# A decoder layer for 16 sequences on one core: first sequence's self attention in half head groups, gelu run twice in place of a cast, maxima of two heads in one transposed tile, and new instruction orders

## Chip, cores and metric

The kernel runs on one core of one Trainium2 chip. The metric is the device time of one launch in microseconds (us), of which the median of several runs is compared. TensorE is PE in the profile's rows, VectorE is DVE, ScalarE is ACT, GpSimd is POOL, and SyncE (SP) issues the DMAs.

## The reference, cut to what matters

One pre-norm decoder layer in float32 for 16 sequences of 256 tokens and 256 features: self attention with 16 heads of 16, cross attention to 77 context rows, and a soft mixture of experts with 8 experts of 128 slots and a hidden size of 1024.

```python
x = x + attn(layernorm(x))                 # softmax(q k^T / 16) v, then Wo
x = x + xattn(layernorm(x), ctx, ctx)      # softmax(q k^T / 4) v, then Wo
xn, se = rms_norm(layernorm(x), gamma_x), rms_norm(slot_embeds, gamma_slot)
logits = einsum('bsd,etd->bset', xn, se)   # 256 tokens x 1024 slots
dispatch = softmax(logits, axis=1)         # over tokens
slots = einsum('bsd,bset->betd', xn, dispatch)
h = gelu(slots @ w1, approximate=False)    # 1024 x 1024
processed = h @ w2
combine = softmax(logits.reshape(b, s, e * t), axis=-1)
x = x + einsum('bnd,bsn->bsd', processed, combine)
```

## The kernel before

**Steps and batches.** A batch is one sequence. Its work is cut into steps with names such as `scores`, `mt`, `shifted`, `ex` and `hidden`, and each engine has its own list of steps. A step name carries a letter for the stage: `c` is self attention, `d` is cross attention and the logits, `m` is the mixture of one batch, `l` is the tail of the mixture. `START` lists the steps of the first pass (self attention of batches 0, 1 and 2, cross attention of 0 and 1, mixture of 0), `ORDER` is the loop body, run 13 times with `c` at batch b+2, `d` at b+1, `m` at b and `l` at b-1, and `FINISH` is the tail. The lists are written out and fix the order on every engine. The engines meet through semaphores that the steps count up and wait on, so a late step holds everything behind it on its engine.

**Matrix products.** The large products are made from three products each of float32 numbers split in two parts, `hi` and `lo`: hi x hi, lo x hi and hi x lo (L453 to L455, one instruction each). ScalarE writes the `hi` part out of PSUM and VectorE or GpSimd subtracts it to make `lo`.

**PSUM.** There are eight banks of 128 x 512. Bank 0 serves the small products of all stages one after another (transposes, `pv`, output projections, keys of the context). Banks 1 to 4 serve a group of four heads' scores and the logits; bank 5 slots, bank 6 and 5 hidden (`hidden_bank`), bank 7 the products `outer` and `combine`.

**Self attention.** A batch has four groups (`quads`, n = 0 to 3) of four heads, on four groups of 32 rows of the array. For each: `scores.n` fills banks 1 to 4; VectorE's `mx.n` takes the maximum of each row (L1122, 2048 elements a partition) and splits it in two; `mt.n` transposes these (L550); `sh.n` adds them to the queries' tile `qz` (L1133), so that `shifted.n` computes keys by queries less the maximum into the same banks (L561); `ex.n` takes the exponent of all four banks into `pt` (L879); `pv.n` multiplies with the values (L574). `scores.n+1` waits for `ex.n`. After `pv.3` come `ml.1`, the normalisation `nrm` (a sum, a reciprocal, two shuffles, two products) and `oproj` (L585). Cross attention does the same with groups of eight heads, `scores2` to `pv2`, in two rounds; there the maxima of even and odd heads lie in two tiles, so `mt2` is four transposes (L638).

**Mixture.** Per batch there are four chunks c of 256 slots. `dispatch.c`, `slots.c`, four steps `hidden.c.q` (12 products each), `outer.c.0` and `outer.c.1` (24 each), `combine.c`. Behind each `hidden.c.q` ScalarE's `ge` writes gelu to `h_f` (L959), VectorE's `hid` casts it to `h_hi` (L1332) and GpSimd's `hid` subtracts in place to `h_lo` (L1456), which `outer` waits for. `hidden.c.2` and `hidden.c.3` wait for the `ge` of two steps earlier, since there are two banks. ScalarE loads a table when it goes from an exponent to gelu or back (L959 and L929 ACT_TABLE_LOAD).

**Fillers.** `idle.n` issues n float32 products of the identity with itself into bank 7 (L811, two records each in the trace), where TensorE would wait otherwise; only in `START`.

## Time and profile before

| what | value |
|---|---|
| runs | 1713.97, 1714.13, 1718.77 us; median 1714.13 us |
| profiled execution, its own time | 1718.86 us |
| its span (first to last instruction) | 1717.1 us |
| mean granted TensorE clock | 0.989 |
| TensorE busy | 1633.2 us, 95% |
| VectorE busy | 1287.0 us, 75% |
| ScalarE busy | 979.1 us, 57% |
| GpSimd busy | 540.1 us, 31% |

The profiled execution took 4.7 us more than the median of the runs, 0.3%. Busy shares are means over the whole span. A matrix product's record is longer than the distance to the next one, since products overlap, so the distance between starts is what a step costs TensorE.

### The profile page before, as it was taken

What the parts mean: (1) busy time and instruction counts of PE and PEld (TensorE: products, weight loads), DVE (VectorE), ACT (ScalarE), POOL (GpSimd) and SP (SyncE); (2) the same over time, 40 slices, a digit from 0 to 9 for tenths busy, and PEclk for the clock granted to TensorE, in tenths of its full rate; (3) what the DMA queues carried; (4) which work ended last, traced back from release to release, by engine and by line L of the source; (5) the groups of instructions that cost most, each with busy time, mean ns of one, the idle gap of its engine ahead of it and who ended that gap; (6) DMA issues with size and microseconds to landing.
All of it is one profiled execution on the core that took longest, in us unless ns stands there. A gap on an engine that the chain in (4) does not pass through costs nothing.

```text
span 1717.1 us, 37771 instructions
## 1 busy us (share of the span) xinstructions
PE 1633.2 (95%) x15552; PEld 1475.2 (86%) x15552; DVE 1287.0 (75%) x2778; ACT 979.1 (57%) x1505; POOL 540.1 (31%) x450
## 2 busy tenths in 40 slices
...
DMA packets 20843, 19.48 MB, mean 11 GB/s; under 512 B 9920, under 2 KB 19776, under 8 KB 20288
## 3 DMA queue, kind: packets, MB, share of 16 engines
...
q14 instruction: 47, 0.39, 0.1%
...
## 4 chain that ended last, share of the span: by engine, by line
PE 79%; DVE 9%; ACT 8%; issue 3%; POOL 1%; DMA 0%; DVEq 0%; SPq 0%; ACTq 0%
PE ps L453 20%; PE ps L454 18%; PE ps L455 18%; PE ps L574 3%; DVE mx L1122 2%; PE ps L561 2%; ACT pt L879 2%; PE ps L541 2%; PE ps L731 2%; PE ps L650 2%; PE ps L585 2%; PE ps L662 2%; PE ps L495 1%; ACT L959 1%; ACT h_f L959 1%
## 5 line engine op out<-in xcount | busy, mean ns | idle before, releaser
L1456 POOL TENSOR_TENSOR h_lo<-h_f,h_hi 128x512 fp32r<-128x512 f32 x256 | 336.3, 1321 | 462.0 <-DVE h_hi L1332 462.0
L453 PE MATMUL ps<-sl_hi,w_hi 128*128 128x256 f32 x1024 | 302.5, 295 | 6.0 <-DVE sl_lo L1014 3.8
L453 PE MATMUL ps<-w_hi,h_hi 128*128 128x256 f32 x1024 | 299.5, 292 | 7.5 <-POOL h_lo L1456 7.5
L454 PE MATMUL ps<-sl_hi,w_lo 128*128 128x256 f32 x1024 | 289.9, 283 | 0.0
L455 PE MATMUL ps<-sl_lo,w_hi 128*128 128x256 f32 x1024 | 289.9, 283 | 0.0
L454 PE MATMUL ps<-w_hi,h_lo 128*128 128x256 f32 x1024 | 289.7, 283 | 0.0
L455 PE MATMUL ps<-w_lo,h_hi 128*128 128x256 f32 x1024 | 289.6, 283 | 0.0
L453 PEld LDWEIGHTS ps<-sl_hi,w_hi 128*128 128x128 f32 x1024 | 196.1, 192 | 32.5 <-issue 16.5
L453 PEld LDWEIGHTS ps<-w_hi,h_hi 128*128 128x128 f32 x1024 | 196.1, 191 | 19.9 <-POOL h_lo L1456 18.3
L959 ACT ACTIVATE h_f<-ps 128x512 f32<-128x512 f32 x256 | 150.6, 596 | 104.6 <-PE ps L455 103.9
L1462 POOL TENSOR_TENSOR cb_lo<-ecomb,cb_hi 128x512 fp32r<-128x512 f32 x60 | 82.0, 1367 | 381.9 <-ACT ecomb L974 381.9
L454 PEld LDWEIGHTS ps<-sl_hi,w_lo 128*128 128x128 f32 x1024 | 196.6, 192 | 0.0
L454 PEld LDWEIGHTS ps<-w_hi,h_lo 128*128 128x128 f32 x1024 | 196.4, 192 | 0.1
L455 PEld LDWEIGHTS ps<-sl_lo,w_hi 128*128 128x128 f32 x1024 | 196.2, 192 | 0.0
L455 PEld LDWEIGHTS ps<-w_lo,h_hi 128*128 128x128 f32 x1024 | 196.1, 191 | 0.0
L1332 DVE CAST h_hi<-h_f 128x512 fp32r<-128x512 f32 x256 | 142.0, 565 | 40.5 <-ACT h_f L959 40.4
L1122 DVE TENSOR_REDUCE mx<-ps 128x8 f32<-128x2048 f32 x64 | 146.2, 2285 | 18.3 <-PE ps L541 18.3
L879 ACT ACTIVATE pt<-ps 128x2048 f32<-128x2048 f32 x64 | 120.1, 1877 | 51.3 <-PE ps L561 51.3
L825 ACT ACTIVATE ds_hi<-ps 128x512 fp32r<-128x512 f32 x64 | 38.2, 598 | 127.7 <-PE ps L731 127.7
L1014 DVE TENSOR_TENSOR ds_lo<-ps,ds_hi 128x512 fp32r<-128x512 f32 x64 | 44.0, 687 | 73.0 <-ACT ds_hi L825 72.9
L959 ACT ACT_TABLE_LOAD x67 | 86.0, 1283 | 15.4 <-PE ps L455 14.3
L825 ACT ACTIVATE lg<-ps 128x512 f32<-128x512 f32 x64 | 38.1, 597 | 92.0 <-PE ps L455 92.0
...
## 6 DMA issues: line engine op xcount, KB each, us to landing
...
```

What stands on the lines that cost most here:

```text
L453: te.matmul(o, lhs[0], rhs[0], start=first, stop=False)
L454: te.matmul(o, lhs[1], rhs[0], start=False, stop=False)
L455: return te.matmul(o, lhs[0], rhs[1], start=False, stop=last)
L574: last = te.matmul(ps[32 * i:32 * i + 32, 0, 0:S], vz[:, j, 8 * c + 2 * i + e, :], pt[:, i, j, :], start=j == 0, stop=j == NT - 1)
L825: return nc.scalar.activation(o, i, ACT.Copy)
L879: nc.scalar.activation(pt[:, :, :, :].rearrange("p i j s -> p i (j s)"), ps[:, 1:1 + R, :], ACT.Exp)\
L959: nc.scalar.activation(h_f[:, 2 * q:2 * q + 2, :], halves(hidden_bank(b, q)), ACT.Gelu).then_inc(s["ge"], 1)
L1014: return V.tensor_tensor(o, a, hi.bitcast(f32), ALU.subtract)
L1122: V.tensor_reduce(mx[:, n, :, :], ps[:, 1:1 + R, :].rearrange("p i (t s) -> p i t s", t=NT), AX, ALU.max, negate=True).then_inc(s["mx"], 1)
L1332: V.tensor_copy(h_hi[:, 2 * q:2 * q + 2, :], h_f[:, 2 * q:2 * q + 2, :]).then_inc(s["h_hi"], 1)
L1456: Q_.tensor_tensor(h_lo[:, part, :], h_f[:, part, :], h_hi[:, part, :].bitcast(f32), ALU.subtract)\
L1462: Q_.tensor_tensor(low[:, :, :], ecomb[:, :, :], hi[:, :, :].bitcast(f32), ALU.subtract).then_inc(s["cb_lo"], 1)
```

## The change

What the core of the diff does, part by part:

1. **Batch 0's self attention** goes by half groups: two heads a step, on one of three pairs of banks (1-2, 3-4, 5-6). `scores`, `mx`, `mt`, `sh`, `shifted` and `ex` get a second number, the half h. A second maxima tile `md_b` and a second `pt_odd` keep neighbours apart. Semaphores whose names begin with `h_` count the first halves.
2. **Normalisation in two parts** (`first_nrm`, `first_nrm2`) for batch 0's self and cross attention: each two groups are normalised by themselves, the first two while the others run.
3. **Gelu twice**: ScalarE writes gelu to `h_hi` and again to `h_f`; VectorE's 256 casts go, and GpSimd waits for ScalarE.
4. **Maxima of cross attention** go into one tile: `mt2` has two transposes in place of four. The masked queries are now made by GpSimd ahead of it (`qm`, two instructions a batch), and `sh2` adds the transposed maxima.
5. **The copy `res` goes** (`keep`): the sum after cross attention lies in two alternating tiles, `x2_even` and `x2_odd`.
6. **The slot embeddings' scaling** (3.6 us on GpSimd, once) goes to ScalarE as eight instructions, `se_mul`.
7. **All four lists** of `START` and `ORDER`, and those of `FINISH`, are new. `START` has fillers in more places: 206 products in place of 152.

```diff
@@ -430,6 +436,19 @@
 
             return (5, 6, 7)[k] if second_batch(a) else 1 + k
 
+        def pt_of(a, n):
+
+            return pt_odd if a == 0 and n % 2 else pt
+
+        def half_banks(n, h):
+
+            at = 1 + 2 * ((2 * n + h) % 3)
+            return slice(at, at + 2)
+
+        def half_sem(name, h):
+
+            return s[name] if h else s["h_" + name]
+
         def hidden_bank(b, q):
 
             return 1 + q if last_batch(b) else 6 - q % 2
...
+                    pe.wait_ge(s["q_sb"], 1)
+                    pe.wait_ge(s["k_lo"], 1)
+                u = 2 * n + h - 3
+                if u >= 0:
+                    pe.wait_ge(half_sem("ex", u % 2), u // 2 + 1)
+                for t in range(NT):
+                    for queries, keys, first in ((qs, k_hi, True), (qz, k_lo, False)):
+                        for i in range(2):
+                            rows = slice(32 * (2 * h + i), 32 * (2 * h + i) + 32)
+                            last = te.matmul(ps[:, half_banks(n, h).start + i, t * S:(t + 1) * S],
+                                             queries[rows, n, t * P:(t + 1) * P], keys[rows, n, :], start=first, stop=not first)
+                last.then_inc(half_sem("s_ps", h), 1)
 
+            def half_mt(n, h):
+
+                misc_free(f"c.mt.{n}.{h}", 0)
+                pe.wait_ge(half_sem("md", h), n + 1)
...
@@ -871,8 +935,18 @@
                 nc.scalar.activation(k_d[:, :, :], k_d[:, :, :], ACT.Identity, scale=half[:, 0:1], bias=half[:, 3:4])\
                     .then_inc(s["k_m"], 1)
 
-            def ex(a, n):
+            def half_ex(n, h):
 
+                act.wait_ge(half_sem("st_ps", h), n + 1)
+                if n >= 2:
+                    act.wait_ge(s["pv"], n - 1)
+                nc.scalar.activation(pt_of(0, n)[:, 2 * h:2 * h + 2, :, :].rearrange("p i j s -> p i (j s)"),
+                                     ps[:, half_banks(n, h), :], ACT.Exp).then_inc(half_sem("ex", h), 1)
+
+            def ex(a, n, *h):
+
+                if h:
+                    return half_ex(n, *h)
                 act.wait_ge(s["st_ps"], nth("st_ps", a, n + 1))
                 if n:
                     act.wait_ge(s["pv"], nth("pv", a, n))
+                nc.scalar.activation(h_hi[:, 2 * q:2 * q + 2, :], halves(hidden_bank(b, q)), ACT.Gelu)
                 nc.scalar.activation(h_f[:, 2 * q:2 * q + 2, :], halves(hidden_bank(b, q)), ACT.Gelu).then_inc(s["ge"], 1)
 
             def pr(b, c):
...
@@ -1116,8 +1198,33 @@
                     last = V.tensor_tensor(vz[:, :, e::2, e * HD:(e + 1) * HD], new[:, :, e::2, :], b_v[:, :, e::2, :], ALU.add)
                 last.then_inc(s["v_sb"], 1)
 
-            def mx_step(a, n):
+            def half_mx(n, h):
+
+                dve.wait_ge(half_sem("s_ps", h), n + 1)
+                of = slice(2 * h, 2 * h + 2)
+                top_sem, hi_sem, top_n, hi_n = (s["mx"], s["md_hi"], n + 1, n + 1) if h else (
+                    s["h_mx"], s["h_mx"], 2 * n + 1, 2 * n + 2)
+                V.tensor_reduce(mx[:, n, of, :], ps[:, half_banks(n, h), :].rearrange("p i (t s) -> p i t s", t=NT), AX,
+                                ALU.max, negate=True).then_inc(top_sem, 1)
+                dve.wait_ge(top_sem, top_n)
+                if n:
+                    dve.wait_ge(half_sem("mt_ps", h), n)
+                top = mx[:, n, of, :].rearrange("p i t -> p t i")
+                V.tensor_copy(md_of[h][:, :, of, HD].bitcast(f32r), top).then_inc(hi_sem, 1)
+                dve.wait_ge(hi_sem, hi_n)
+                V.tensor_tensor(md_of[h][:, :, of, HD + 1], top, md_of[h][:, :, of, HD], ALU.subtract).then_inc(half_sem("md", h), 1)
+
...
@@ -1142,8 +1251,24 @@
                 V.scalar_tensor_tensor(xo[:, c, :], odd, half[:, 1:2], xo[:, c, :], ALU.mult, ALU.add)\
                     .then_inc(s["ml"], 1)
 
-            def nrm(a):
+            def first_nrm(a, c):
+
+                step = "rl" if c else "la"
+                dve.wait_ge(s["ml"], nth("ml", a, 2 * c + 1))
+                V.stream_shuffle(od[:, c, :], lsum[:, c, :], [8 * c + HD * (1 - r // HD) for r in range(2 * HD)])\
+                    .then_inc(s["ls"], 1)
+                dve.wait_ge(s["ls"], nth("ls", a, c + 1))
+                V.reciprocal(od[:, c, :], od[:, c, :]).then_inc(s[step], 1)
+                dve.wait_ge(s[step], nth(step, a, 1))
+                dve.wait_ge(s["ml"], nth("ml", a, 2 * c + 2))
+                last = V.tensor_tensor(od[:, c, :], xo[:, c, :], od[:, c, :], ALU.mult)
+                if c:
...
-                    last = V.tensor_reduce(md2[:, :, e, :, HD * (1 - e)].rearrange("p t i -> p i t"), every[:, :, :, e, :],
+                    last = V.tensor_reduce(md2[:, :, :, HD * (1 - e)].rearrange("p t i -> p i t"), every[:, :, :, e, :],
                                            AX, ALU.max, negate=True)
                 last.then_inc(s["md2"], 1)
 
             def sh2_step(a, c):
 
                 dve.wait_ge(s["mt2_ps"], nth("mt2_ps", a, c + 1))
+                dve.wait_ge(s["q2_m"], nth("q2_m", a, 1))
                 for e in range(2):
-                    last = V.scalar_tensor_tensor(sh2[:, e, :], q2[:, c, :], half[:, e:e + 1],
-                                                  ps[:, 0, e * S:(e + 1) * S], ALU.mult, ALU.add)
+                    last = V.scalar_tensor_tensor(sh2[:, c, e, :], ps[:, 0, 0:S], half[:, 1 - e:2 - e],
+                                                  sh2[:, c, e, :], ALU.mult, ALU.add)
                 last.then_inc(s["sh2"], 1)
 
             def ml2(a, c):
...
@@ -1450,8 +1580,16 @@
                     last = Q_.tensor_scalar(kms2[:, :, e, :], km2[:, :, e, :], half[:, 4 + e:5 + e], None, ALU.add)
                 last.then_inc(s["kms2"], 1)
 
+            def qm(a):
+                pool.wait_ge(s["q2_sb"], nth("q2_sb", a, 1))
+                if later(a):
+                    pool.wait_ge(s["st2_ps"], nth("st2_ps", a - 1, C))
+                for e in range(2):
+                    last = Q_.tensor_scalar(sh2[:, :, e, :], q2[:, :, :], half[:, e:e + 1], None, ALU.mult)
+                last.then_inc(s["q2_m"], 1)
...
-        m.slots.2 m.outer.1.1 c.mt.1 m.hidden.2.0 c.shifted.1 m.hidden.2.1 c.scores.2 c.pv.1 m.hidden.2.2 m.hidden.2.3
+        m.slots.2 m.outer.1.1 c.mt.1 c.shifted.1 m.hidden.2.0 m.hidden.2.1 c.scores.2 c.pv.1 m.hidden.2.2 m.hidden.2.3
```

**TensorE in the first pass**, behind the first scores of batch 0. `md` holds the maxima, `qs`/`k_hi` and `qz`/`k_lo` the two parts of queries and keys, `consts` by itself is a filler. Before:

```order
L541 MATMUL ps<-k_lo,qz 128x256 x4
L811 MATMUL ps<-consts 128x128 x11
L550 MATMUL ps<-consts,md 128x128 [waits s_md,s_xt1_lo]
L550 MATMUL ps<-consts,md 128x128
L811 MATMUL ps<-consts 128x128
L561 MATMUL ps<-qs,k_hi 128x256 [waits s_sh]
L561 MATMUL ps<-qs,k_hi 128x256 x3
L561 MATMUL ps<-qz,k_lo 128x256 x4
L561 MATMUL ps<-qs,k_hi 128x256 x4
L561 MATMUL ps<-qz,k_lo 128x256 x4
```

After, the first half group's transposes and shifted scores, then the second's transposes:

```order
L875 MATMUL ps<-consts 128x128 x4
L590 MATMUL ps<-consts,md 128x128 [waits s_h_md,s_xt1_lo]
L590 MATMUL ps<-consts,md 128x128
L875 MATMUL ps<-consts 128x128 x6
L601 MATMUL ps<-qs,k_hi 128x256 [waits s_h_sh]
L601 MATMUL ps<-qs,k_hi 128x256
L601 MATMUL ps<-qz,k_lo 128x256 x2
L601 MATMUL ps<-qs,k_hi 128x256 x2
L601 MATMUL ps<-qz,k_lo 128x256 x2
L590 MATMUL ps<-consts,md_b 128x128 [waits s_md,s_h_sh]
L590 MATMUL ps<-consts,md_b 128x128
L875 MATMUL ps<-consts 128x128 x3
```

A step has half as many products, other halves stand between, and the fillers are cut in smaller pieces.

**ScalarE in the loop**, first chunk of the mixture, from the second gelu step to the exponent of cross attention (`q` and `k_d` belong to other stages, `edt` is the exponent for `dispatch`). Before:

```order
L959 ACTIVATE h_f<-ps 128x512 [waits s_h_ps]
L895 ACTIVATE q_109<-ps,bcol 128x256 [waits s_od2,s_q2_ps]
L895 ACTIVATE q_109<-ps,bcol 128x256
L825 ACTIVATE k_hi<-k_d 128x1024 [waits s_k_d]
L871 ACTIVATE k_d<-k_d,half 128x1024 [waits s_k_h]
L959 ACTIVATE h_f<-ps 128x512 [waits s_h_ps] x2
L929 ACT_TABLE_LOAD
L929 ACTIVATE edt,csum<-lg,cm 128x256 [waits s_cm]
L929 ACTIVATE edt,csum<-lg,cm 128x256
L906 ACTIVATE pt_114<-ps,mkc 77x2048 [waits s_st2_ps]
```

After:

```order
L1033 ACTIVATE h_hi<-ps 128x512 [waits s_h_ps]
L1034 ACTIVATE h_f<-ps 128x512
L1033 ACTIVATE h_hi<-ps 128x512 [waits s_h_ps]
L1034 ACTIVATE h_f<-ps 128x512
L889 ACTIVATE k_hi<-k_d 128x1024 [waits s_k_d]
L935 ACTIVATE k_d<-k_d,half 128x1024 [waits s_k_h]
L1033 ACTIVATE h_hi<-ps 128x512 [waits s_h_ps]
L1034 ACTIVATE h_f<-ps 128x512
L1003 ACT_TABLE_LOAD
L1003 ACTIVATE edt,csum<-lg,cm 128x256 [waits s_cm]
L1003 ACTIVATE edt,csum<-lg,cm 128x256
L980 ACTIVATE pt_116<-ps,mkc 77x2048 [waits s_st2_ps]
```

Each gelu is two instructions, and the third gelu step moved ahead of the two instructions on `k_hi` and `k_d`.

**VectorE in the loop**, around the last group of self attention (`qz` is `sh.3`, `xh_d` the third normalised input, `sl_lo` and `pr_lo` the low parts of slots and processed slots, `total` the sum for `combine`). Before:

```order
L1133 TENSOR_TENSOR qz<-ps,qz 128x256 [waits s_mt_ps]
L1052 TENSOR_TENSOR sc_143<-pw_d 128x2 [waits s_ln3_pw]
L1054 TENSOR_SCALAR sc_143<-sc_143 128x2 [waits s_ln3_sc]
L1057 RECIPROCAL sc_143<-sc_143 128x2 [waits s_ln3_sc]
L1059 SCALAR_TENSOR_TENSOR sc_143<-sc_143,pw_d 128x2 [waits s_ln3_sc]
L1064 TENSOR_SCALAR xh_d<-x_86,mv_d,sc_143 128x256 [waits s_ln3_sc]
L1064 TENSOR_SCALAR xh_d<-x_86,mv_d,sc_143 128x256
L1014 TENSOR_TENSOR sl_lo<-ps,sl_hi 128x512 [waits s_sl_hi]
L1014 TENSOR_TENSOR pr_lo<-ps,pr_hi 128x512 [waits s_pr_hi]
L1307 TENSOR_TENSOR total<-total,ecomb 128x256 [waits s_sm,s_cb_hi]
L1307 TENSOR_TENSOR total<-total,ecomb 128x256 [waits s_sm]
L1014 TENSOR_TENSOR xd_lo<-ps,xd_hi 128x512 [waits s_xt3_hi]
```

After:

```order
L1096 TENSOR_TENSOR sl_lo<-ps,sl_hi 128x512 [waits s_sl_hi]
L1134 TENSOR_TENSOR sc_145<-pw_d 128x2 [waits s_ln3_pw]
L1136 TENSOR_SCALAR sc_145<-sc_145 128x2 [waits s_ln3_sc]
L1139 RECIPROCAL sc_145<-sc_145 128x2 [waits s_ln3_sc]
L1141 SCALAR_TENSOR_TENSOR sc_145<-sc_145,pw_d 128x2 [waits s_ln3_sc]
L1146 TENSOR_SCALAR xh_d<-x_odd,mv_d,sc_145 128x256 [waits s_ln3_sc]
L1146 TENSOR_SCALAR xh_d<-x_odd,mv_d,sc_145 128x256
L1242 TENSOR_TENSOR qz<-ps,qz 128x256 [waits s_mt_ps]
L1442 TENSOR_TENSOR total<-total,ecomb 128x256 [waits s_sm,s_cb_hi]
L1442 TENSOR_TENSOR total<-total,ecomb 128x256 [waits s_sm]
L1096 TENSOR_TENSOR pr_lo<-ps,pr_hi 128x512 [waits s_pr_hi]
```

`sl_lo` and `xh_d` went ahead of `qz`, and the two sums went ahead of `pr_lo`.

## Rows read from the trace of the kernel before

**Rows 1.** the page: the span
```profile
span 1717.1 us, 37771 instructions
```

**Rows 2.** busy time by stretch; us, busy (xinstructions) by engine, granted clock, DMA
```profile
23.32:59.51 36.19, 28.12 (x334) 22.41 (x335) 21.59 (x36) 14.19 (x20) 7.43 (x5) 0.97 0.10 18
59.51:79.41 19.90, 14.83 (x68) 11.65 (x69) 9.14 (x28) 2.61 (x5) 5.28 (x6) 0.59 0.07 20
...
115.16:134.00 18.84, 16.81 (x138) 15.19 (x139) 10.19 (x19) 8.21 (x13) 0.00 (x0) 0.82 0.01 2
134.00:245.39 111.39, 95.33 (x924) 81.94 (x923) 82.47 (x175) 59.62 (x86) 31.36 (x26) 0.97 0.02 6
...
845.31:945.28 99.97, 98.26 (x955) 88.96 (x954) 79.09 (x173) 59.91 (x92) 32.68 (x27) 1.00 0.03 8
1545.77:1717.10 171.33, 151.91 (x1274) 145.46 (x1272) 95.98 (x191) 85.43 (x143) 60.22 (x46) 0.99 0.02 6
```

**Rows 3.** timeline, first head group of batch 0; start, us, engine, line
```profile
23.32 0.40 PE L541 MATMUL ps<-k_hi,qs 32*128 32x256 f32 x4 [0.57 <-DVE qs L1090]
...
24.11 2.29 DVE L1122 TENSOR_REDUCE mx<-ps 128x8 f32<-128x2048 f32 x1 [1.05 <-PE ps L541]
...
27.43 0.42 DVE L1133 TENSOR_TENSOR qz<-ps,qz 128x256 fp32r<-128x256 f32 x1 [0.60 <-PE ps L550]
...
28.71 1.88 ACT L879 ACTIVATE pt<-ps 128x2048 f32<-128x2048 f32 x1 [3.84 <-PE ps L561]
```

**Rows 4.** timeline, end of batch 0's self attention
```profile
53.71 1.07 PE L574 MATMUL ps<-pt,vz 128*32 128x256 f32 x16 [0.99 <-ACT pt L879]
...
56.15 1.75 DVE L1150 RECIPROCAL lsum<-lsum 128x256 f32<-128x256 f32 x1
...
59.51 3.75 PE L585 MATMUL ps<-wo,od 128*128 128x256 f32 x8 [4.15 <-DVE od L1160]
```

**Rows 5.** timeline of the loop, ScalarE between two gelu steps and the next exponent
```profile
865.93 1.07 ACT L825 ACTIVATE k_hi<-k_d 128x1024 fp32r<-128x1024 f32 x1
...
868.19 0.58 ACT L959 ACTIVATE h_f<-ps 128x512 f32<-128x512 f32 x1
...
869.69 1.28 ACT L929 ACT_TABLE_LOAD   x1
...
872.65 1.97 ACT L906 ACTIVATE pt<-ps,mkc 77x2048 f32<-77x2048 f32 x1 [0.56 <-PE ps L650]
```

**Rows 6.** timeline of the loop, TensorE: maxima transposes and what follows them
```profile
881.05 0.39 PE L550 MATMUL ps<-consts,md 128*128 128x128 f32 x2
881.95 0.39 PE L561 MATMUL ps<-qs,k_hi 32*128 32x256 f32 x4 [0.52 <-DVE qz L1133]
...
882.63 1.07 PE L662 MATMUL ps<-pt,v2z 77*32 77x256 f32 x16
...
890.54 0.60 PE L638 MATMUL ps<-consts,md 128*128 128x128 f32 x4
890.89 0.36 PE L453 MATMUL ps<-pr_hi,cb_hi 128*128 128x256 f32 x1
...
904.12 0.38 PE L550 MATMUL ps<-consts,md 128*128 128x128 f32 x2
904.25 0.36 PE L453 MATMUL ps<-sl_hi,w_hi 128*128 128x256 f32 x1
```

**Rows 7.** the page's costliest groups: the residual, the gelu and the cast
```profile
L1456 POOL TENSOR_TENSOR h_lo<-h_f,h_hi 128x512 fp32r<-128x512 f32 x256 | 336.3, 1321 | 462.0 <-DVE h_hi L1332 462.0
...
L959 ACT ACTIVATE h_f<-ps 128x512 f32<-128x512 f32 x256 | 150.6, 596 | 104.6 <-PE ps L455 103.9
...
L1332 DVE CAST h_hi<-h_f 128x512 fp32r<-128x512 f32 x256 | 142.0, 565 | 40.5 <-ACT h_f L959 40.4
```

**Rows 8.** timeline of the loop: VectorE behind a GpSimd instruction, and GpSimd's
```profile
926.62 1.71 DVE L1064 TENSOR_SCALAR xh_d<-x,mv_d,sc 128x256 f32<-128x256 f32 x2
...
926.56 1.29 POOL L1462 TENSOR_TENSOR cb_lo<-ecomb,cb_hi 128x512 fp32r<-128x512 f32 x1 [0.96 <-ACT ecomb L974]
```

More of the change, by code:

```diff
@@ L93 @@
-        c1.shifted.3 d1.kv c1.pv.3 m0.outer.0.0 m0.dispatch.1 c1.oproj m0.outer.0.1 m0.slots.1 m0.hidden.1.0 c2.xt.1
-        m0.hidden.1.1 d1.xt.2 c2.k c2.q m0.hidden.1.2 m0.hidden.1.3 c2.v m0.combine.0 d1.q2 c2.scores.0 m0.outer.1.0
-        m0.dispatch.2 c2.mt.0 c2.shifted.0 m0.slots.2 m0.outer.1.1 d1.scores2.0 m0.hidden.2.0 d1.mt2.0 m0.hidden.2.1
-        d1.shifted2.0 c2.pv.0 m0.hidden.2.2 d1.scores2.1 d1.pv2.0 m0.combine.1 d1.mt2.1 d1.shifted2.1 m0.hidden.2.3
-        c2.scores.1 d1.pv2.1 m0.dispatch.3 c2.mt.1 c2.shifted.1 c2.scores.2 c2.pv.1 m0.outer.2.0 c2.mt.2 c2.shifted.2
@@ L98 @@
-        m0.slots.3 c2.scores.3 d1.oproj2 m0.outer.2.1 c2.mt.3 c2.pv.2 c2.shifted.3 d1.xt.3 m0.hidden.3.0 m0.hidden.3.1
-        m0.hidden.3.2 c2.pv.3 d1.logits.0 m0.hidden.3.3 d1.logits.1 m0.combine.2 c2.oproj d1.logits.2 d1.logits.3
+        s0.idle.12 c0.xt.1 s0.idle.13 c0.k c0.q s0.idle.7 c0.v s0.idle.16 c0.scores.0.0 c0.scores.0.1 c0.scores.1.0
+        s0.idle.4 c0.mt.0.0 s0.idle.6 c0.shifted.0.0 c0.mt.0.1 s0.idle.3 c0.scores.1.1 c0.shifted.0.1 c0.mt.1.0
+        s0.idle.3 c0.scores.2.0 s0.idle.2 c0.shifted.1.0 c0.pv.0 s0.idle.4 c0.mt.1.1 c0.scores.2.1 c0.shifted.1.1
@@ new lines @@
+        d0.pv2.1 s1.idle.11 c1.mt.0 s1.idle.2 c1.shifted.0 s1.idle.7 d0.oproj2 c1.scores.1 c1.pv.0 s1.idle.7 c1.mt.1
+        s1.idle.4 c1.shifted.1 s1.idle.6 d0.xt.3 s1.idle.6 d0.logits.0 d0.logits.1 d0.logits.2 d0.logits.3
+        m0.dispatch.0 c1.scores.2 c1.pv.1 m0.slots.0 s1.idle.5 c1.mt.2 s1.idle.2 c1.shifted.2 m0.hidden.0.0
+        m0.hidden.0.1 c1.scores.3 c1.pv.2 m0.hidden.0.2 m0.rxt s1.idle.2 c1.mt.3 s1.idle.2 c1.shifted.3 d1.kv
+        m0.hidden.0.3 c1.pv.3 s1.idle.4 m0.rmb m0.outer.0.0 c1.oproj m0.dispatch.1 m0.outer.0.1 m0.slots.1 c2.xt.1
```

311 lines of the change are left out of this document (179 added, 132 removed).

## The prediction

> **What bounds the kernel now.** I read the page first, for the span [rows 1], then busy time by stretch, cut where the lists of steps change [rows 2], and then timelines of single places. The reader is to see three different regimes in [rows 2]. The loop takes 99.97 us a batch with TensorE busy for 98.26 of them at full clock; between 245.39 and 1545.77 us lie 13 such passes (1300.4 us). What is left there to gain is what TensorE issues, and its short waits. The first pass, up to 245.39, is another matter: batch 0's self attention takes 36.19 us in which TensorE's 28.12 busy us are mostly fillers, the next 19.90 us ran at a mean granted clock of 0.59, and 115.16 to 134.00 at 0.82. The tail takes 171.33 us with 151.91 busy.
>
> In the first pass each head group is one chain [rows 3]: scores at 23.32, the maxima on VectorE for 2.29 us, the addition to the queries at 27.43, the exponent on ScalarE at 28.71 for 1.88 us, and only then the next scores. It ends with `pv.3` at 53.71, the reciprocal at 56.15 for 1.75, and `oproj` at 59.51, whose 8 records take 3.75 us at the lower clock [rows 4]. In the loop the same chains are covered by the mixture's products.
>
> The profiled execution's own time is 1718.86 us for a span of 1717.1; the median of the runs is 1714.13, 4.7 us lower. I make the sum in the profiled execution's time and take the difference off the median.
>
> **The change part by part.**
>
> *Half groups in batch 0.* A half group costs VectorE about half of 2.29 us, two small splits of about 0.2 each (from the start of the maxima to the addition are 3.3 us, of which 2.29 are the maxima and the rest these splits and the transposes) and an addition of 0.42 [rows 3]: some 2.0 us. Eight are 16 us. With the rest of VectorE's list in this stretch (first normalisation half 2.6, the sums behind `pv.1` 0.9, mask and a weight's low part 1.3) it is 20.8 us, so from 24.1 the last half's addition is done near 45.8. Then one half of `shifted`, half an exponent (0.95) and latencies put `pv.3` at about 47.6 in place of 53.71: 6.1 us less. If instead ScalarE held it (eight half exponents at 0.95, plus the scaling of the embeddings, now 8 instructions of about 0.4, and the weights' conversions) it would be 1 to 3 us later; if nothing but VectorE's maxima counted, 4 us earlier. I take 6.1.
>
> *Normalisation in halves.* From `pv.3` to `oproj` are now 5.8 us [rows 4]. After the change only the second half's shuffle, reciprocal (1.75) and product lie behind the sums: 1.0 + 0.95 + 2.6 + latency, 4.7. It saves 1.1. For cross attention the first half's 2.6 us go ahead of an addition that `shifted2.1` waits for, so there I count a loss of 1.0 and a gain of 1.1.
>
> *Fillers and clock.* In 59.51 to 79.41 TensorE was busy 14.83 us at 0.59. At full clock the same work takes 14.83 x 0.59 = 8.7, 6.1 less, nearly all on the chain, since in this stretch each product is waited for. The new list has fillers ahead of `oproj` and between all small steps there, where before it had none. I take 4.5 of the 6.1 (below: 0, should the clock fall all the same). For 115.16 to 134.00, 16.81 x (1 - 0.82) = 3.0; I take 2.5.
>
> *Rest of the first pass.* From 134.00 to 245.39, 111.39 us hold 95.33 busy at 0.97. So 16 us are waits and 3 are clock. VectorE loses 16 casts here (565 ns each on the mean [rows 7]), and the queries and keys of batch 2 come ahead of the second chunk. I take 5 of the 19, with 0 and 11 as bounds.
>
> *Loop: two transposes fewer twice a batch.* Four transposes hold TensorE from 890.54 to 890.89, 0.35 us; two from 904.12 to 904.25, 0.13 [rows 6]. That is 0.22 twice, 0.44 a batch. The work that makes up for it, `qm` on GpSimd, is two instructions of 128 x 512, near 1.3 us each by the subtraction of that size [rows 7]; GpSimd is busy 32.68 of 99.97 us and 35.3 after it, and its `q2` is ready some 4 us before `sh2.0` needs the result. It costs nothing; were it late, `shifted2.0` would wait for it.
>
> *Loop: gelu twice.* One gelu takes 596 ns and the cast 565 on the mean [rows 7]. The second gelu starts 0.5 us after the first (as two ScalarE instructions of that size follow each other), the cast came some 0.1 after it and took about as long. So GpSimd's subtraction starts as early as before. ScalarE goes from 59.9 to about 68 us a batch, VectorE from 79.1 to about 69.7 (16 casts at 0.56 and the copy). Two things hang on ScalarE. First, bank 5 or 6 is released 0.5 us later: `hidden.c.3` has 1.44 us of TensorE work in between, and where a table load (1.28, [rows 5]) comes before, I find 0.0 to 0.2 us of wait at `hidden.1.3`. Second, the chain to the next exponent. Now the gelu step at 868.19 comes behind 2.3 us on the keys (865.93 on), then comes the table load at 869.69, and the exponent at 872.65 begins after a wait of 0.56 for TensorE [rows 5]. After the change, from the end of `hidden.0.2`: gelu 1.1, keys 2.3, gelu 1.1, load and `edt` 2.4, exponent 2.0, latencies 0.1, 9.0 us. TensorE's own work over the same steps takes 8.9 (two thirds of it `hidden.0.3`, `outer.0.0` and `combine.3`, 48 products of 0.12). So ScalarE just takes over there, and the first 0.22 of the transposes is not gained.
>
> *Loop: new places.* `mt.1` is now followed at once by `shifted.1`. Where the loop does this already, the shifted scores start 0.90 us after the transposes (881.05 and 881.95 [rows 6]), 0.77 more than the 0.13 that these need. In return `hidden.2.0` stands between `shifted.1` and `scores.2`, which waited 0.6 for the exponent; and `scores.3`, which waited 0.4, has three steps before it. At the end, `xh.3` and the sums go ahead of `pr_lo`: I find `combine.2` waiting 0.3. Sum: -0.44 + 0.2 + 0.77 - 0.6 - 0.2 - 0.4 + 0.3, about -0.4 a batch, -5 over 13. As this is a sum of differences each good to 0.2, I keep -13 and +9 for the range.
>
> The instruction on `xh_d` that took 1.71 us for two [rows 8] ended when GpSimd's `cb_lo` did (926.56 + 1.29 = 927.85), and the second of the two needed only 0.4. In the new order GpSimd has no instruction at that time, so `xh.3` goes ahead of `sh.3` at a cost of 1.6 us and not 2.6. The Trainium skill has this rule too ("SBUF — State Buffer", section "SBUF: two separate sides": VectorE in its two-port modes and GpSimd take one pair of ports as a lock, and the loser waits for the whole instruction); the trace agrees, 1.3 us lost beside a GpSimd instruction of 1.29. By that rule removing 256 casts also removes 256 chances to wait, in my sum already through their mean of 565 ns.
>
> *Tail.* It gets the same edits: -0.44, the casts' queueing gone, and gelu pairs on a ScalarE that is busy half the time. I take -1, from -4 to +3.
>
> The sum: -6.1 - 1.1 - 4.5 + 1.0 - 1.1 - 2.5 - 5 - 5 - 1 = -25.3. The profiled execution would come to 1693.6, the median to **1689 us**.
>
> **The rivals.**
>
> *A. The loop gains all.* If there is no wait where I find 0.3 and 0.2, nor the 0.2 at `scores.0`, the loop gives 0.6 to 1.0 us a batch more than I took, 8 to 13 in all: 1676 to 1681. For it speaks VectorE's 9 us of freed time, which makes its answers earlier everywhere; against it, that TensorE is idle for only 1.7 us a batch now (99.97 less 98.26).
>
> *B. The loop gives nothing or loses a little.* Gelu pairs sit in more places than I followed. With 0.5 us more a batch than in my sum the loop is at +0.1: 1696; with 1.0 more, 1702.
>
> *C. Half groups cost TensorE as much as whole ones.* Four products on four row groups run together: 16 records take from 881.95 to 882.63, 0.68 us [rows 6]. Two at a time would take as long for half the work, so scores and shifted take 8 x 1.3 = 10.7 in place of 5.4 us, and with eight pairs of transposes (1.1), four `pv` (4.0) and 49 fillers of two records of 0.09 (8.8) TensorE has 25 us from first scores to `pv.3`'s end, as many as I have for VectorE's chain. Where the two alternate, the gain shrinks by 3 to 4 us, and if the clock falls as before, by 4.5 more: 1697. The Trainium skill gives the rule on which this stands ("TensorEngine Tiling (Array Packing)", theoretical speedup: a dimension of 32 gives up to 4 tiles at a time); half a group uses two of the four.
>
> *D. Slower.* ScalarE becomes what ends each chunk: a `ge` pair behind a table load, an exponent and `xo2` releases its bank later than TensorE asks. The price is 0.5 us for each gelu pair not covered. It decides from 2.0 us a batch over my sum, that is when one pair in four loses its whole 0.5: 13 x 2.0 = 26 eats what the first pass gains, and at 2.6 the time is 1723. Against it: ScalarE is at 68 of 100 us, and before the exponent in [rows 5] it had 0.56 to spare.
>
> *E. No change.* The loop is 1.6 to 2.3 us a batch over my sum and gives back what the first pass gains: 1710 to 1719.
>
> **How the numbers follow.** My forecast with its neighbourhood (1683 to 1695) has 0.45, A 0.15, B 0.20, C 0.12, D 0.04, E 0.04. The range goes from A's 1675 to B with C, 1704, and leaves out 0.2. A measurement of this kernel tells 0.3%, 5 us, from no change. All of the forecast, A, B and C are faster than that: 0.92. E is the same, 0.04, D slower, 0.04.
>
> **What would show it.** Half groups: `oproj` of batch 0 starting near 52 us, and `pv.3` near 48. Clock: granted 0.9 or more from there to the first logits. First pass: the loop starting near 225 us. Loop: 99.6 us a batch, ScalarE at 68 and VectorE at 70 busy us; waits of TensorE for `qz` three times a batch, and for the exponent of cross attention (`pt`, the 77-row one) at `scores.0`. Wrong would be a loop over 100.5 or under 98.8, TensorE waiting for gelu (`h_f`) by over 0.5 us a batch, or a clock that falls again before `oproj`.

## The result, and the profile after

| | before | after |
|---|---|---|
| median of four runs | 1715.72 us (1713.97 to 1718.77) | 1703.66 us (1702.69 to 1706.44) |
| profiled execution, its own time | 1718.86 us | 1702.69 us |
| loop starts at | 245.39 us | 238.12 us |
| one pass of the loop | 99.97 us | 99.47 us |
| from the loop's end to the last instruction | 171.3 us | 169.8 us |

The ratio is 0.9926, 95% interval 0.9913 to 0.9939: 12 to 13 us less, where the forecast was 25. The 1703.66 us lie at the upper end of the stated range (1675 to 1704). The page of the changed kernel begins (span; then busy time and share by engine):

```profile
span 1700.9 us, 37966 instructions
...
PE 1635.1 (96%) x15604; PEld 1479.4 (87%) x15604; DVE 1170.5 (69%) x2522; ACT 1103.4 (65%) x1773; POOL 580.4 (34%) x482
```

Busy time by stretch, with the columns of [rows 2] (the fifth number with an x is GpSimd, then the granted clock):

```profile
23.32:59.51 36.19, 34.13 (x331) 27.90 (x332) 27.88 (x55) 17.55 (x26) 10.22 (x9) 1.00 0.08 14
59.51:79.41 19.90, 19.51 (x198) 16.82 (x197) 14.76 (x40) 8.05 (x14) 8.41 (x8) 1.00 0.07 20
79.41:115.16 35.75, 30.64 (x274) 25.81 (x274) 22.47 (x44) 14.11 (x17) 1.04 (x1) 0.86 0.01 2
115.16:134.00 18.84, 18.24 (x200) 15.16 (x198) 12.33 (x21) 12.11 (x19) 3.78 (x3) 1.00 0.00 1
134.00:238.12 104.12, 91.88 (x859) 79.41 (x858) 69.24 (x153) 62.42 (x94) 30.43 (x25) 0.97 0.03 7
835.00:934.47 99.47, 97.74 (x950) 88.62 (x949) 71.97 (x156) 67.35 (x108) 35.59 (x29) 1.00 0.04 8
```

The loop is close to what the forecast said (99.6 us a pass; ScalarE 68, VectorE 70 busy). Its list of TensorE's waits in this pass is one line, three waits for `qz`, as forecast; the wait forecast at `scores.0` isn't there:

```profile
PE ps L625 <- DVE qz L1242: 1.6, 3, 0.5
```

The gain that is missing is in the first pass. I wrote down for each step of TensorE when it starts in either trace; the difference is the lead of the changed kernel. The last column is the best variant, told below. The first row is no part of the change: executions whose lists are the same up to there begin batch 0's first scores anywhere from 21.83 to 23.16 us, so 1.3 us of every lead in the fourth column come from that start.

| step | before | after | lead | lead forecast | lead of `e13_holes` |
|---|---|---|---|---|---|
| first scores of batch 0 | 23.32 | 22.03 | 1.3 | 0 | 1.5 |
| batch 0's `pv.3` | 53.71 | 49.96 | 3.8 | 6.1 | 3.9 |
| `oproj` | 59.51 | 55.81 | 3.7 | 7.2 | 4.9 |
| `scores2.1` | 86.61 | 76.93 | 9.7 | 11.7 | 10.9 |
| first logits | 115.16 | 111.23 | 3.9 | 11.8 | 8.8 |
| batch 1's `scores.3` | 134.32 | 127.24 | 7.1 | 14.3 | 12.0 |
| loop | 245.39 | 238.12 | 7.3 | 19.3 | 13.5 |

The lead is built up until `scores2.1` and then more than halved by the logits. Most of what happened there is in the clock (stretches of that place, columns as above):

```profile
80.00:84.00 4.00, 2.60 (x22) 2.32 (x20) 3.93 (x8) 3.26 (x4) 0.00 (x0) 1.00 0.02 4
84.00:86.00 2.00, 1.10 (x16) 0.55 (x16) 1.85 (x4) 1.49 (x2) 0.00 (x0) 0.90 0.00 0
86.00:88.00 2.00, 0.47 (x8) 0.50 (x12) 1.38 (x2) 1.27 (x1) 0.00 (x0) 0.50 0.00 0
88.00:92.00 4.00, 4.00 (x39) 2.51 (x35) 3.09 (x5) 0.84 (x2) 0.00 (x0) 0.50 0.00 0
92.00:96.00 4.00, 4.00 (x21) 4.00 (x21) 0.43 (x2) 0.00 (x0) 0.00 (x0) 0.52 0.00 0
```

From 80 on TensorE was busy for 3.7 us of 5.6, with no filler around `c1.v`, `d0.shifted2.1` and `c1.scores.0`; then, at 85.6, the clock fell to 1.2 GHz. It was still there when 11 fillers came up: `mt.0`'s maxima were ready near 91.5, the fillers ran until 95.4. Before, fillers stood between these steps and the clock was full from 84 to 100 us. I call a wait of TensorE without fillers a hole. A second fall after a hole from 160.94 to 163.52 lasted until about 167.5, a third came at 178.

And the end of batch 0's attention (timeline: start, length, engine, line; the third row is the weights' low part on GpSimd):

```profile
49.96 1.07 PE L638 MATMUL ps<-pt_odd,vz 128*32 128x256 f32 x16
...
51.45 3.07 PE L875 MATMUL ps<-consts 128*128 128x128 f32 x26
...
51.66 5.13 POOL L1630 TENSOR_TENSOR w_lo<-g_w,w_hi 128x512 fp32r<-128x512 f32 x4 [22.43 <-ACT w_hi L889]
...
52.44 1.75 DVE L1261 RECIPROCAL od<-od 128x256 f32<-128x256 f32 x1
54.23 1.44 DVE L1264 TENSOR_TENSOR od<-xo,od 128x256 f32<-128x256 f32 x1
55.81 1.97 PE L649 MATMUL ps<-wo,od 128*128 128x256 f32 x8 [1.29 <-DVE od L1264]
```

Two things are to be seen. The product into `od` takes 1.44 us beside GpSimd's 5.13, where the same instruction elsewhere takes 0.43. And 13 fillers (26 records) take 3.07 us, 0.236 each.

### The profile page after: what moved, and what is told of

Read it like the earlier page. It is cut to its first block, busy times and chain, and to the rows that moved or that the text cites. A ratio compares the mean times of both kernels' runs of the same rounds, so it can differ in the third digit from the quotient of the medians.

```text
span 1700.9 us, 37966 instructions
## 1 busy us (share of the span) xinstructions
PE 1635.1 (96%) x15604; PEld 1479.4 (87%) x15604; DVE 1170.5 (69%) x2522; ACT 1103.4 (65%) x1773; POOL 580.4 (34%) x482
## 4 chain that ended last, share of the span: by engine, by line
PE 72%; POOL 10%; DVE 8%; issue 5%; ACT 4%; DMA 0%; DVEq 0%; SPq 0%; ACTq 0%; POOLq 0%
PE ps L472 18%; PE ps L474 16%; PE ps L473 16%; POOL h_lo L1594 5%; PE ps L638 4%; POOL sh L1588 3%; PE ps L625 2%; PE ps L564 2%; DVE mx L1229 2%; PE ps L725 2%; PE ps L794 2%; PE ps L736 2%; PE ps L649 2%; PE ps L875 1%; DVE qz L1242 1%
## 5 line engine op out<-in xcount | busy, mean ns | idle before, releaser
L1594 POOL TENSOR_TENSOR h_lo<-h_f,h_hi 128x512 fp32r<-128x512 f32 x256 | 331.5, 1303 | 408.6 <-ACT h_f L1034 405.7
L1033 ACT ACTIVATE h_hi<-ps 128x512 fp32r<-128x512 f32 x256 | 153.7, 600 | 60.0 <-PE ps L474 58.0
L1229 DVE TENSOR_REDUCE mx<-ps 128x8 f32<-128x2048 f32 x60 | 137.2, 2287 | 43.9 <-PE ps L564 43.7
L953 ACT ACTIVATE pt<-ps 128x2048 f32<-128x2048 f32 x60 | 112.4, 1873 | 47.0 <-PE ps L625 46.9
L1033 ACT ACT_TABLE_LOAD x67 | 86.0, 1283 | 15.5 <-PE ps L474 14.3
L889 ACT ACTIVATE sl_hi<-ps 128x512 fp32r<-128x512 f32 x64 | 37.9, 593 | 84.5 <-PE ps L474 84.4
```

What stands on the lines that cost most here:

```text
L889: return nc.scalar.activation(o, i, ACT.Copy)
L953: nc.scalar.activation(pt[:, :, :, :].rearrange("p i j s -> p i (j s)"), ps[:, 1:1 + R, :], ACT.Exp)\
L1033: nc.scalar.activation(h_hi[:, 2 * q:2 * q + 2, :], halves(hidden_bank(b, q)), ACT.Gelu)
L1229: V.tensor_reduce(mx[:, n, :, :], ps[:, 1:1 + R, :].rearrange("p i (t s) -> p i t s", t=NT), AX, ALU.max, negate=True).then_inc(s["mx"], 1)
L1594: Q_.tensor_tensor(h_lo[:, part, :], h_f[:, part, :], h_hi[:, part, :].bitcast(f32), ALU.subtract)\
```

## The experiments

All times are medians; the changed kernel has 1703.66. Because of the differing start of batch 0's scores, steps are compared from the first scores on where that is said.

**Clock alone, in the kernel before** (`e4_before_fillers`): 44 fillers more.

```diff
-c0.oproj d0.kv s0.se_transp.1.0 d0.xt.2 d0.q2 c1.xt.1
+s0.idle.13 s0.idle.12 c0.oproj s0.idle.3 d0.kv s0.idle.8 s0.se_transp.1.0 d0.xt.2 s0.idle.6 d0.q2 s0.idle.2 c1.xt.1
```

> The kernel before with 44 fillers added from 54 to 76 us and nothing else changed: what the clock alone is worth. Theory (between 59.51 and 79.41 all steps are a chain through TensorE at 0.59 of its clock): granted clock 1.0 there, d0.scores2.0 4 to 6 us earlier than 77.06; as later waits take some of it, 1711 to 1713 in place of 1715.7. Rival (VectorE and the latencies set the pace, the clock is idle talk): d0.scores2.0 within 1 us of 77.06, time the same.

The stretch from `oproj` (60.11) on, in place of 0.59 of the clock in [rows 2]:

```profile
60.11:80.00 19.89, 17.73 (x152) 15.14 (x150) 12.85 (x36) 7.64 (x10) 8.71 (x9) 1.00 0.08 20
```

`d0.scores2.0` came at 72.43 in place of 77.06, the loop at 240.31 in place of 245.39 (of both differences 0.6 us is an earlier start of the first scores). `oproj` itself comes 1.2 us later than before by that measure, behind its 25 new fillers; from there to `scores2.1` the fillers save 7.0 us. Two short falls of the clock, at 110 and 124 us, remain. The median fell by 2.2 us only (1713.08 beside 1715.29, ratio 0.9983, 0.9973 to 0.9993). From the first scores to the loop, fillers without any half group give 4.5 of the 6.0 us that the change gives by the same measure; in the medians the part is smaller.

**Whole groups in the changed kernel** (`e3_whole`): `c0.scores.n` to `c0.ex.n` as before, with fillers in every wait.

> The changed kernel with batch 0's self attention in whole groups again, fillers in between, all else as changed. Theory (half groups gave 3.75 us at pv.3, and what they gave reaches the end only in part, as the later list gives back a lead): pv.3 near 53.7, the loop starts 1 to 4 us later than 238.12, time 1705 to 1708. If the forecast's 6.1 us for half groups was right and something else held pv.3 back, pv.3 comes near 56. Rival (half groups give nothing, since they need twice as many records): pv.3 at 50 to 51 and the time at 1703.7.

From first scores to `pv.3` 30.86 us, in place of 27.93: half groups give 2.9 us there, not 6.1. Beside the kernel before, which takes 30.39 us with other fillers, they give 2.5. The loop starts 1.3 us later, the median is 1706.98.

**GpSimd's weights out of the way** (`e2_lo4`):

```diff
-c0.bias.1 s0.lo.4 d0.rstd.2 c1.rstd.1 c1.bias.1 d0.km d0.qm d0.bias.2 d0.rstd.3
+c0.bias.1 d0.rstd.2 c1.rstd.1 c1.bias.1 d0.km d0.qm d0.bias.2 s0.lo.4 d0.rstd.3
```

> The changed kernel with GpSimd's four subtractions of weights (s0.lo.4, 51.66 to 56.79 us) moved behind d0.bias.2. Theory (VectorE's product into od took 1.44 us in place of 0.43 because it ran beside them): that product takes 0.43, oproj starts at 54.8 in place of 55.81, and what follows comes 1.0 us earlier up to d0.scores2.1; of the whole time 0 to 1 us. Rival (the length belongs to the product's output of this place, not to its neighbour): 1.44 and 55.8 as before.

```profile
54.63 0.42 DVE L1264 TENSOR_TENSOR od<-xo,od 128x256 f32<-128x256 f32 x1
...
55.20 1.97 PE L649 MATMUL ps<-wo,od 128*128 128x256 f32 x8 [0.28 <-DVE od L1264]
```

From `pv.3` to `oproj` 4.83 us in place of 5.85: the theory holds. 1702.37 us, the loop 1.5 us earlier; a part of this is that the fall of the clock at 86 us lasted 6.8 us in this execution and 10.2 in that of the changed kernel.

**Fillers in the holes, first try** (`e1_fillers`, `e5_second_gap`):

```diff
-d0.mt2.1 c1.v d0.shifted2.1 c1.scores.0
+d0.mt2.1 s0.idle.10 c1.v d0.shifted2.1 s1.idle.14 c1.scores.0
```
```diff
-m0.hidden.1.2 c2.scores.0 ... m0.dispatch.2 d1.mt2.0 ... d1.shifted2.0 m0.outer.1.1
+m0.hidden.1.2 m0.pad.18 c2.scores.0 ... m0.dispatch.2 m0.outer.1.1 d1.mt2.0 ... d1.shifted2.0
```

> The changed kernel with 24 more fillers in the first pass: 10 ahead of c1.v and 14 ahead of c1.scores.0, where TensorE idled for 1.5 and 2.4 us before its granted clock was 0.5 from about 86 to 95.7 us. Theory (the clock fell because the new order has no fillers there, and c1.mt.0 then waited behind 11 fillers at half clock): the clock stays at 1.0 from 80 to 96, c1.mt.0 starts near 91.6 in place of 95.40, the loop starts 3 to 4 us earlier than at 238.12, the time is about 1700. Rival (VectorE's list of normalisation, values and low parts sets the pace there, the clock costs nothing): c1.mt.0 moves by under 1 us and the time stays at 1703.7.

> The changed kernel with 18 fillers ahead of c2.scores.0 (on the mixture's free output bank) and m0.outer.1.1 moved up ahead of d1.mt2.0, for the two later places where TensorE idled (160.94 to 163.52 us and 175.9 to 177.6) and the granted clock was 0.5 after it. Theory (these two falls cost the lead that was lost between c2.scores.0, 10.9 us ahead of before, and d1.shifted2.1, 5.0 ahead): clock 1.0 from 164 to 182, the loop starts 2 to 4 us earlier than 238.12, time 1700 to 1702. Rival (the chain there runs through ScalarE: gelu behind the queries of batch 2): the clock is mended, but the loop starts within 1 us of 238.12, time 1703.7.

The clock was mended at both places, and both theories failed in their numbers: 1703.54 and 1702.99 us, the loop at 237.52 and 238.51. Counted from the first scores the loop comes 1.5 and 0.6 us earlier than in the changed kernel, where 3 to 4 and 2 to 4 were expected. I had counted 0.12 us a filler; at 0.236 the 10 held `c1.v` back by 2.2 us, and ScalarE's queries behind it, and the 18 held `c2.scores.0` until 165.12, 2.1 after its queries were there.

**Holes filled to size** (`e13_holes`), with the weights moved as in `e2_lo4`:

```diff
-d0.shifted2.1 c1.scores.0 d0.pv2.1 s1.idle.11 c1.mt.0
+d0.shifted2.1 s1.idle.9 c1.scores.0 d0.pv2.1 s1.idle.6 c1.mt.0
-m0.hidden.1.2 c2.scores.0
+m0.hidden.1.2 m0.pad.10 c2.scores.0
```

> The changed kernel with GpSimd's weights moved behind d0.bias.2, and fillers sized to the two holes by their measured 0.236 us: 9 behind d0.shifted2.1 (hole of 2.3 us), 6 in place of 11 behind d0.pv2.1, 10 ahead of c2.scores.0 (hole of 2.5 us). The 14, 10 and 18 of the earlier runs overfilled the holes. Theory (two clock falls and the shared port are where the lead went): c1.mt.0 near 90.5 in place of 95.40, d0.logits.0 near 107, c2.scores.0 2 us earlier still, the loop starts at 233 to 235, time 1698 to 1700. Rival (later waits give it back whatever the clock): the loop starts at 236.6 or later, as with the weights moved alone, time 1702.4.

```profile
79.73:106.34 26.61, 22.65 (x236) 18.35 (x236) 19.59 (x38) 11.15 (x11) 1.04 (x1) 1.00 0.01 2
106.34:158.00 51.66, 48.59 (x445) 43.72 (x446) 35.10 (x81) 32.79 (x52) 11.81 (x11) 1.00 0.04 9
158.00:170.00 12.00, 11.09 (x122) 9.89 (x120) 7.74 (x14) 7.41 (x14) 6.94 (x5) 1.00 0.01 2
200.00:210.00 10.00, 8.50 (x71) 6.38 (x64) 4.97 (x8) 3.51 (x4) 2.50 (x2) 0.83 0.01 2
```

`c1.mt.0` at 90.67, the logits at 106.34, the loop at 231.85; one fall is left in the first pass, at 204. **1697.40 us** (1696.27 to 1700.67), ratio 0.9889, 0.9872 to 0.9906: faster than both kernels (the ratio is to the kernel before). So 19 fillers more, 5 fewer, and one step moved take 6 us off the changed kernel.

**What holds the half groups** (`e9_swap`, `e10_swap_semul`, `e12_thin`, `e14_holes_thin`). In `e9_swap` the second half's transposes go ahead of `pv` (shown for one of three groups; on VectorE `sh.2.1` also goes ahead of `ml.0`); `e10` moves the embeddings' scaling too; `e12` cuts the 49 fillers up to `pv.3` to 22.

```diff
-c0.shifted.1.0 c0.pv.0 s0.idle.4 c0.mt.1.1
+c0.shifted.1.0 c0.mt.1.1 s0.idle.4 c0.pv.0
```

> The changed kernel with each second half's transposes (c0.mt.1.1, mt.2.1, mt.3.1) ahead of pv of the group before instead of behind it. Theory (what held pv.3 at 49.96 in place of the forecast 47.6 is output bank 0, which pv and the transposes share: mt.1.1 waited for ScalarE's copy xo.0, mt.2.1 for VectorE's ml.0, mt.3.1 for xo.1, and VectorE idled 1.60, 0 and 0.68 us for it): pv.3 1.5 to 2.5 us earlier, near 48, time -1 to -2. Rival (the fillers in between held it, or ScalarE's own list with the scaling of the embeddings at 37.21 to 40.50): pv.3 moves by under 0.7 us.

> As the kernel with the swapped transposes, and the scaling of the embeddings on ScalarE (3.3 us) moved behind the exponent c0.ex.2.0, which waited for it from 38.57 to 40.40. Theory (both banks and ScalarE's list hold the chain): pv.3 another 0.5 to 1.5 us earlier than with the swap alone. Rival (the exponent then waits elsewhere: the 3.3 us are behind another one): no difference to the swap alone.

> The changed kernel with the 49 fillers between the first scores and pv.3 cut to 22. A filler takes 0.236 us (26 records, two a filler, in 3.07 us at full clock), so TensorE's list there is scores and shifted 10.8 us, transposes 2.2, pv 4.2, fillers 11.6: 28.8 for the 27.93 us it takes. Theory (TensorE's list itself is what holds the half groups, of which I had put fillers at 0.18): 6.4 us of fillers less give pv.3 1.5 to 3 us earlier, near 47.6 from the same start, clock still 1.0, time -1 to -3. Rival (the fillers lie in waits for VectorE's maxima and ScalarE's exponents, which set the pace): pv.3 within 0.5 us of 49.96. Second rival: the clock falls with fewer of them, and oproj comes 2 us or more later.

The theory of bank 0 fell: `pv.3` came 29.53 us after the first scores, not 27.93 (1704.66 us), and 29.54 with the scaling moved (1704.54). Counted from the first scores the addition `sh.1.1` did come 1.6 us earlier, but `scores.2.1` then waited for `pv.0`, and `pv.2` for an addition that stands behind 2.7 us of normalisation on VectorE. `e12_thin` got its second rival:

```profile
22.80:28.00 5.20, 3.80 (x46) 3.18 (x47) 4.29 (x8) 1.64 (x9) 3.29 (x3) 1.00 0.57 94
28.00:46.00 18.00, 17.33 (x118) 12.23 (x117) 8.92 (x23) 9.15 (x16) 1.80 (x3) 0.53 0.03 7
```

With 27 fillers fewer the clock is 0.53 for 18 us, `pv.3` comes 32.95 us after the first scores, 1707.87 us. As the clock fell, this run does not tell whether TensorE's list with its 49 fillers or the waits hold the half groups. The 22 fillers in the kernel with its holes filled (`e14_holes_thin`) cost 4.9 us again (1702.26).

**The loop: parts at old and new places.** The changed operations with the loop's steps at the places of before; in `e6_old_places` the product for the queries (`qm`) stands behind the third subtraction of GpSimd, in `e6b` all of GpSimd's list is that of the changed kernel. Then each part alone; `e16` and `e17` also have the tail's order of before.

```diff
 e15, in the kernel before:
+nc.scalar.activation(h_hi[...], halves(hidden_bank(b, q)), ACT.Gelu)
-V.tensor_copy(h_hi[...], h_f[...])
 e16 (loop in the order of before) and e17 (new order), in the changed kernel from batch 1 on:
-nc.scalar.activation(h_hi[...], halves(hidden_bank(b, q)), ACT.Gelu)
+V.tensor_copy(h_hi[...], h_f[...])
```

> The changed kernel, first pass and tail as changed, with the loop's steps at their places of before (the casts, the copy of the residual and nothing else taken out of VectorE's list, the product for the queries put into GpSimd's). It has the single maxima tile and gelu twice, but not the new places. By the forecast's sum the operations give 0.44 less 0.2 a pass and the new places 0.13 to 0.2: a pass of 99.7 us, time about 1707. Rival 1 (the operations give all, the places nothing): 99.5 us a pass, 1703.7. Rival 2 (with the old places gelu twice holds ScalarE's list up and the new places are what makes it pay): over 100 us, 1710 or more.

> The loop's steps of before with the changed operations, as in the run with 107 to 108 us a pass, but GpSimd's list as in the changed kernel, so that the product for the queries comes ahead of the second subtraction and not behind the third. In that run shifted2.0 waited 4 us for it. Theory (that place alone made the pass 7.5 us longer): a pass of 99.5 to 99.9 us, time 1704 to 1709. Rival (the gelu pairs, for which the old places leave no time on ScalarE, cost several us a pass): over 101 us a pass.

> The kernel before, in its own order, with gelu twice on ScalarE in place of gelu and cast, and nothing else changed. By the forecast's sum this part gives 0 to 0.4 us a pass to the bad: 100.0 to 100.4, time 1716 to 1721. Theory from the run with the old places (103 to 104.6 us a pass, shifted2.0 and hidden.0.2 waiting): ScalarE's list before the exponent of cross attention is what breaks, so 102 to 104 us a pass, time 1742 to 1770.

> The changed kernel's first pass, and from batch 1 on the order of before with gelu once and the cast on VectorE, the single maxima tile with its product on GpSimd as the only change there (the copy of the residual is gone too). By the forecast's sum: two transposes fewer twice a pass, 0.44 us, of which 0.2 is lost: 99.5 to 99.8 a pass. Rival (the product on GpSimd, 3.1 us and not 2.6, comes between the addition for the keys and the subtractions and shifted2.0 waits for it): 100.5 or more.

> The changed kernel with its loop's new places, but gelu once and the cast back on VectorE from batch 1 on, each cast behind the instruction of VectorE that stood ahead of it in the order of before; the tail in the order of before. Theory (the new places are made for the two gelus and VectorE's free 9 us; with the casts back they lose): 99.8 to 102 us a pass. Rival (the places give the 0.5 us by themselves, and gelu twice is a cost that they hide): 99.4 us or less a pass.

| order of the loop | gelu | maxima tile | us a pass | median, us |
|---|---|---|---|---|
| before | once, cast | two | 99.97 | 1715.7 |
| before (`e15`) | twice | two | 101.7 | 1741.72 |
| before, `qm` ahead of the subtractions (`e16`) | once, cast | one | 106.9 to 108.0 | 1819.99 |
| before, `qm` behind the third (`e6`) | twice | one | 106.9 to 108.2 | 1808.34 |
| before, GpSimd's new (`e6b`) | twice | one | 102.1 to 104.6 | 1756.22 |
| new (`e17`) | once, cast | one | 105.5 to 106.6 | 1804.83 |
| new (the change) | twice | one | 99.47 | 1703.66 |

Every mixture is slower than both ends. In `e6` and `e16` a part of that is the clock, which falls once in each pass, for 3.4 or 6.8 us, where TensorE waits as the rows below show; from 455 to 1300 us its mean is 0.98 and 0.97, in `e6b` 0.99, in `e15` and `e17` 1.00. So the 5.5 to 6.6 us of `e17` are lost without the clock. What `e6_old_places` waited for at `shifted2.0` (VectorE, then GpSimd):

```profile
915.40 0.88 DVE L1337 SCALAR_TENSOR_TENSOR sh<-ps,half,sh 128x256 f32<-128x256 f32 x2 [4.87 <-POOL sh L1588]
...
910.92 1.29 POOL L1594 TENSOR_TENSOR h_lo<-h_f,h_hi 128x512 fp32r<-128x512 f32 x1 [2.64 <-ACT h_f L1034]
912.19 3.11 POOL L1588 TENSOR_SCALAR sh<-q,half 128x512 f32<-128x512 f32 x2
```

In `e16_tile_only`, with `qm` ahead of the subtractions, it is the other way round: four subtractions in a row come behind it, and `outer.0.0` for them (GpSimd, then TensorE):

```profile
905.69 3.11 POOL L1598 TENSOR_SCALAR sh<-q,half 128x512 f32<-128x512 f32 x2 [4.07 <-DVE h_hi L1476]
908.76 1.46 POOL L1584 TENSOR_TENSOR x<-x,biases 128x512 f32<-128x512 f32 x1
910.19 7.13 POOL L1606 TENSOR_TENSOR h_lo<-h_f,h_hi 128x512 fp32r<-128x512 f32 x4
...
917.37 0.58 PE L477 MATMUL ps<-w_hi,h_hi 128*128 128x256 f32 x1 [5.46 <-POOL h_lo L1606]
```

TensorE's waits of one pass of `e15_gelu_only` (us in total, times, longest): the query copy of cross attention comes late because a gelu pair stands ahead of it on ScalarE (880.85 us, where the pair began at 879.90), and two exponents and a gelu are late too; for these two I did not follow the chain.

```profile
PE ps L615 <- ACT q L887: 0.9, 1, 0.9
PE ps L533 <- ACT pt L871: 0.8, 2, 0.5
PE ps L445 <- ACT h_f L952: 0.7, 1, 0.7
```

## Why the prediction was wrong, by its steps

- **"Half groups in batch 0", 6.1 us.** Mis-sized: 2.9 us by `e3_whole`. The count of VectorE's work was right (20.8 us; its records from 22.81 to 47.93 hold 20.5), though 24.1 and 20.8 make 44.9 and not the 45.8 of the forecast. What the sum left out is that VectorE also waits 4.6 us for TensorE. Rival C had this: a half group's scores take 0.58 us from start to start (28.22 to 28.80 below), a whole group's 0.68 [rows 6]. The Trainium skill ("TensorEngine Tiling (Array Packing)", theoretical speedup) gives a speedup of up to 4 times for a dimension of up to 32; by the trace two row groups at a time reach little more than half of what four do. C also had fillers at 0.18 us, where they take 0.236, and TensorE is busy for 27.33 of the 27.93 us from the first scores to `pv.3`, 49 fillers included. I gave C 12%, and only its cost without the fall of the clock came true. Which wait would have to go first stays open: the two tries at it (`e9_swap`, `e10_swap_semul`) found others of the same size behind them, and `e12_thin` lost the clock.

```profile
28.22 0.39 PE L581 MATMUL ps<-k_hi,qs 32*128 32x256 f32 x2
...
28.80 0.28 PE L601 MATMUL ps<-qs,k_hi 32*128 32x256 f32 x2
```

- **"Normalisation in halves", 1.1 us.** 0 us. The working was right but for a neighbour: `s0.lo.4` had been moved on GpSimd to just here. `e2_lo4` shows the 1.0 us. I had written of exactly this lock at `xh_d` [rows 8], and did not look along GpSimd's list for where the change puts it.
- **"Fillers and clock", 4.5 us.** Right and a little low: from `oproj` to `scores2.1` the lead grows by 6.0, at full clock. `e4_before_fillers` shows that the fillers alone do it (7.0 us over the same steps).
- **The step that failed** is the one that claims a clock of 0.9 or more from there to the first logits. I counted fillers where the new list has them and not where the old list has them and the new one doesn't: from 79.41 to 115.16, where the mean clock was 0.86, I took 0.1 us of gain, and 5.8 were lost. From `scores2.1` to the logits the kernel before takes 28.6 us, the changed one 34.3, and `e13_holes`, with 9 fillers in the hole and 5 fewer behind it, 30.6: 3.7 of the 5.8 come back. Runs whose lists are those of the changed kernel up to the logits show that 2.3 us of it at least are the clock: the fall lasted 10.2 us in the profiled execution above, 6.8 in `e6`, `e6b`, `e16` and `e17`, and 3.4 in `e5_second_gap`, and the same steps took 34.3, 33.0 to 33.3, and 32.0 us. So the execution above is the worst of them. Of the last 1.4 us, down to 30.6, the 5 fewer fillers can be up to 1.2. The other 2.1 us are lost at full clock as well: 1.2 up to `c1.scores.0`, where `shifted2.1` waits 1.5 us for an addition behind the first half's normalisation (forecast 1.0), 1.0 gained back at `oproj2` (forecast 1.1), and 1.8 from there to the logits, which no run takes apart.
- **"115.16 to 134.00", 2.5 us.** Right: 3.1.
- **"Rest of the first pass", 5 us.** 0.2 us, near the lower bound named (0). Its 16 us of waits were a number without a mechanism. In `e13_holes` this stretch gives 1.5 us. (The terms up to the loop make 19.3 us, which is a loop from 226 and not from 225.)
- **Loop, 0.4 us a pass.** Measured 0.50: 7.4 us over 13 passes for 5. TensorE's busy time falls from 98.26 to 97.74 us, the size of the transposes' 0.44, and what it idles stays at 1.7. That the other terms came to nothing together was luck, as the sum added parts as if each stood alone. "It costs nothing" for `qm` holds only at its place: it takes 3.1 us and not 2.6, and is ready 0.9 us before `sh2.0` starts, not 4. The instruction on `xh_d` [rows 8] had lost 1.0 us and not 1.3 (1.39 in place of 0.41); as forecast, it is free of its neighbour now and takes 0.41. Gelu twice costs 1.7 us a pass at the old places, where I had 0 to 0.4 for any.
- **Tail, 1 us.** Measured 1.6, but executions of one list differ there by as much: 165.8 us from the loop's end to TensorE's last step without a short fall of the clock near 1688, 167.3 with it. The kernel before has such a fall at 1621, so its 1.6 us more can be that alone.
- **The base.** Of 14.7 us between forecast and median, 9.1 are the steps above (25.3 less 16.2); without the earlier first scores, 1.3 us of luck, they would be 10.4. The other 5.6 come from the 4.7 us that I took off for the profiled execution of before, which lies that much over its median, while that of after lies 1.0 under its own.
